# The expert weights of a second feed-forward block, laid out in DRAM as four pieces of a partition's row in place of one

## The chip, the core and the metric

One core of a Trainium2 chip runs the whole program in one launch. The metric is device time in microseconds (us). The core has five engines that run side by side and meet only at semaphores: TensorE (PE; its weight loads are PEld), VectorE (DVE), ScalarE (ACT), GpSimd (POOL) and SyncE (SP). DMAs are issued from a queue of SP (q1 in the profile), of ACT (q10) or of POOL (q0); all of them are carried out by the same 16 DMA engines. A DMA over 128 partitions gives each DMA engine 8 partitions.

## The reference

Two layers, each an attention block and a mixture of experts. Only the second mixture is touched. For 2048 rows `x` of 256 numbers it computes

```python
logits = silu(x @ rw1 + rb1) @ rw2 + rb2
k_logits, k_index = top_k(logits, 2)
k_prob = softmax(k_logits)
for e in range(8):
    we = sum(where(k_index == e, k_prob, 0))
    out += we[:, None] * (silu(x @ w1[e] + b1[e]) @ w2[e] + b2[e])
```

with `w1[e]` of 256 x 1024 and `w2[e]` of 1024 x 256, all in float32. "First layer weights" below are `w1` and `b1`.

## The kernel before

The second mixture is the last stage of the program. The router's table sorts the 4096 pairs of row and expert into 39 tiles (`NT1`) of up to 128 rows; a tile belongs to one expert. The first 8 tiles are those of the experts 0 to 7; which expert each of the other 31 belongs to is read from the table at run time.

For each tile:

- GpSimd gathers its 128 rows of 1 KB from DRAM by an indirect DMA (`fetch`, line 1354) into one of four buffers, four tiles ahead.
- SyncE loads the expert's first layer weights (`load_up`, line 1503) into one of two buffers `W1`: 128 partitions of 8224 bytes, 1028 KB. Of these 2056 floats a partition, 2048 are `w1` and 8 are `b1`. The load of tile i+2 goes into the buffer of tile i, so it waits until ScalarE has finished tile i (line 1498; the bias columns are read from the same buffer). From the ninth tile on SyncE then reads the expert's number into a register, which is the address of the load.
- TensorE transposes the gathered rows (line 333), multiplies by `w1` in two halves of 16 matmuls (`up`, line 457), and by `w2`, which lies in SBUF for all eight experts (`down_parts`, lines 483 to 486). The order on TensorE is fixed: up of half c, transposes of the next tile, down of half c-1.
- ScalarE applies silu with the bias (line 1213), VectorE splits the result into a high and a low part (lines 951, 953) and later adds the bias of the second layer and weighs the rows (lines 976 to 978).
- GpSimd adds the tile's 128 rows to the output in DRAM by an indirect accumulating DMA (`give`, line 1361). Two tiles can hold the same row, so each such scatter waits until the one before it has landed. GpSimd's order is: give of tile i, fetch of tile i+4.

In DRAM the weights of expert e are rows e*128 to e*128+127 of an array of 2056 columns, so a partition's 8224 bytes are one contiguous run, and SyncE's DMA copies rows to partitions.

The first mixture has the same structure with tiles of 2 MB and 1 MB of weights (`wide` is then `WS`), and gives rows out by a plain scatter into `yd`.

Of the kernel before, what the change touches and what calls it, by code (L numbers as in the profile page):

```python
# [15 lines left out]
P = 128  # L16
# [6 lines left out]
E = 8  # L23
# [53 lines left out]
def build(nc, cst, x, ctx_2048, plen, kmask, g_xattn, g_ffn, W_in, b_in, g_res, g_init, rw0, rb0, w01, w02,  # L77
          att_b, rw1, rb1, rw2, rb2, w11, w12, b12, out):
    es = ExitStack()
    with es:  # L80
# [11 lines left out]
        def placed(name, shape, at, dt=F32):  # L92
            return nc.alloc_sbuf_tensor_at(name, shape, dt, offset=arena + 4 * at)[:, :]

        def sem(name):
            return es.enter_context(nc.semaphore(name))
# [22 lines left out]
        W1 = [placed(f"W1{i}", [P, 2056], x_at + 2056 * i) for i in range(2)]  # L119
# [11 lines left out]
        def scratch(name, rows):  # L131
            return nc.dram_tensor(name, [rows, D], F32, kind="Internal").ap()


        dep_d, xn0, xn1, yd = (scratch(n, r) for n, r in (
            ("dep_d", NK * P), ("xn0", P + T), ("xn1", P + T), ("yd", P + T)))
# [3 lines left out]
        def sm(n):  # L140
            at[0] += n
            assert at[0] <= SMN, at[0]
            return SM[:, at[0] - n:at[0]]
# [11 lines left out]
        tile, lane, tabp, row = sm(2 * NC), sm(2 * NC), sm(40), sm(2 * NC)  # L155
# [16 lines left out]
        zero = Z1[:, 3584:3840]  # L172
# [15 lines left out]
        def w2_half(s, raw=False):  # L188
# [25 lines left out]

        d_plen, d_cst, d_ck, d_v, d_first, d_small = (sem(n) for n in ("d_plen", "d_cst", "d_ck", "d_v", "d_first", "d_small"))
        d_x = [sem(f"d_x{g}") for g in range(4)]
        d_zero = [sem("d_zero0"), sem("d_zero1")]
        d_dep = [sem(f"d_dep{i}") for i in range(2)]
        d_dg = [sem(f"d_dg{i}") for i in range(4)]
        d_xn = [[sem(f"d_xn{l}{i}") for i in range(4)] for l in range(2)]  # L220
        d_up = [[sem(f"d_up{l}{i}") for i in range(2)] for l in range(2)]
# [14 lines left out]
        v_xn, t_xn, a_xt, t_lg = sem("v_xn"), sem("t_xn"), sem("a_xt"), sem("t_lg")  # L236
        v_la, a_ex, v_oh, t_rank, v_slot, t_tab, v_tab, v_eid = (
            [sem(f"{n}{l}") for l in range(2)] for n in ("v_la", "a_ex", "v_oh", "t_rank", "v_slot", "t_tab", "v_tab", "v_eid"))
        v_flag, t_flag, v_mbh, v_ka, t_ka = (sem(n) for n in ("v_flag", "t_flag", "v_mbh", "v_ka", "t_ka"))

        t_tr, a_tr, t_up, t_down, v_y = (
            [sem(f"{n}{l}") for l in range(2)] for n in ("t_tr", "a_tr", "t_up", "t_down", "v_y"))
# [27 lines left out]
        def landed(i, slots):  # L270
            return 16 * (i // slots + 1)
# [51 lines left out]
        def _(e):  # L323
# [90 lines left out]
            def tables(l):  # L414
                nt, cc = (NT0, NT1)[l], NC * (1 + l)
                lanes, _, vals = slot_table(l)
                for q in range(cc):
                    if q % 8 == 0:
                        e.wait_ge(v_slot[l], q // 8 + 1)
                    t = e.matmul(PB[6][:, 0:3 * nt + 3], lanes[:, q, :], vals[:, q, :, :].rearrange("p s t -> p (s t)"),  # L420
                                 start=q == 0, stop=q == cc - 1)
                t.then_inc(t_tab[l], 1)
# [731 lines left out]
        def _(e):  # L1154
# [2 lines left out]
            e.wait_ge(v_pad, 2)  # L1157
            e.dma_start(CK[0:REM, 12, :], ctx_2048[12 * P:S2, 0:D]).then_inc(d_ck, 16)
            e.wait_ge(p_set, 1)
            for l, buf in ((0, xn0), (1, xn1)):  # L1160
                e.dma_start(buf[0:P, :], zero).then_inc(d_zero[l], 16)


            trash = [WS[0][:, 0:D], WS[0][:, D:2 * D]]
# [156 lines left out]
        def _(e):  # L1321
# [28 lines left out]
            def experts(l, nt, xn, into, **add):  # L1350
                def fetch(i):
                    if i >= 4:
                        e.wait_ge(t_tr[l], bank_of["xt", l, i - 4])
                    e.indirect_dma_start(FXL[i % 4], None, xn, bass.IndirectOffsetOnAxis(  # L1354
                        ap=tabi[:, i:i + 1].bitcast(U32), axis=0)).then_inc(d_xl[l][i % 4], 16)

                def give(i):
                    e.wait_ge(v_y[l], i + 1)
                    if i:
                        e.wait_ge(d_y[l][(i - 1) % 2], landed(i - 1, 2))  # L1360
                    e.indirect_dma_start(into, bass.IndirectOffsetOnAxis(ap=tabi[:, i:i + 1].bitcast(U32), axis=0),  # L1361
                                         FY[i % 2], None, **add).then_inc(d_y[l][i % 2], 16)

                e.wait_ge(v_tab[l], 1)
                for z in d_zero:
                    e.wait_ge(z, 16)
                for i in range(4):
                    e.wait_ge(d_xn[l][i], landed(NC - 1, 4))
                for i in range(4):
                    fetch(i)  # L1370
                if l == 1:
                    w2_low(14)
                    w2_low(15)
                for i in range(nt):
                    give(i)
                    if i + 4 < nt:
                        fetch(i + 4)

            def w2_low(s):
                e.wait_ge(a_wh[1], s + 1)  # L1380
                e.tensor_tensor(w2_half(s)[:, :, 1, :], w2_half(s, raw=True)[:, :, 1, :],
                                w2_half(s)[:, :, 0, :].bitcast(F32), ALU.subtract).then_inc(p_wl, 1)

            experts(0, NT0, xn0, yd)


# [66 lines left out]
            for s in range(14):  # L1453
                w2_low(s)
            e.wait_ge(d_res, 64)
            experts(1, NT1, xn1, out, compute_op=ALU.add)
            for i in range(2):
                e.wait_ge(d_y[1][i], landed(NT1 - 1 - (NT1 - 1 - i) % 2, 2))
# [3 lines left out]
        def _(e):  # L1462
# [23 lines left out]
            def experts(l, nt, w_up, w_down, free):  # L1486
                up_n = 4 * FF if l == 0 else 2 * FF + 8
                wide = WS if l == 0 else W1
                regs = {}

                def row(i, n):
                    return bass.ds(regs[i] * n, n) if i >= E else slice(i * n, i * n + n)

                def load_up(i):
                    if i >= 2:
                        e.wait_ge(t_up[l], (2 - l) * 2 * (i - 1))
                        if l == 1:
                            e.wait_ge(a_h, 4 * (i - 1))
                    if i >= E:
                        if i == E:  # L1500
                            e.wait_ge(v_eid[l], 1)
                        regs[i] = e.value_load(eidi[0:1, i:i + 1], min_val=0, max_val=E - 1)
                    e.dma_start(wide[i % 2][:, 0:up_n], w_up[row(i, P), :]).then_inc(d_up[l][i % 2], 16)

                def load_down(i):
                    if i >= 2:
                        e.wait_ge(v_wl, 2 * (i - 2) + 2)
                    e.dma_start(WS[i % 2][:, 4096:6144], w_down[row(i, P), :]).then_inc(d_down[i % 2], 16)

                def load_whole(k):  # L1510
                    x = W2_ORDER[k]
                    e.dma_start(W2G[E - 1 - x].rearrange("p (j s n) -> p j s n", j=8, s=2)[:, :, 1, :],
                                w_down[row(x, P), :].rearrange("p (j n) -> p j n", j=8)).then_inc(d_w2[k % 4], 16)

                if l == 1:
                    for k in range(4):
                        load_whole(k)
                    free()
                    load_up(0)
                    e.dma_start(B2, b12.partition_broadcast(P)).then_inc(d_bias, 16)  # L1520
                    e.wait_ge(t_hr, 32)
                    for i in range(4):
                        e.wait_ge(d_xn[1][i], landed(NC - 1, 4))
                    for k in range(4, E):
                        load_whole(k)
                    e.wait_ge(t_tab[1], 1)
                    for i in range(1, nt):
                        load_up(i)
                    return

                for i in range(2):
                    free(i)
                    load_up(i)
                    load_down(i)
                for c in range(1, 2 * nt + 1):
                    i = c // 2
                    if c % 2:
                        if i + 2 < nt:
                            load_up(i + 2)
                    elif i + 1 < nt:  # L1540
                        load_down(i + 1)
# [104 lines left out]
```

## Time and profile before

| | us |
|---|---|
| median of 3 runs | 1243.98 (1239.08 to 1245.86) |
| the profiled execution | 1242.3 |
| its span, first to last instruction | 1240.5 |

The profile is of one execution. "Busy" is the time in which an engine carries out instructions; "idle before" a group is the time in which its engine did nothing just before them, with what ended it. A DMA's "us to landing" runs from its issue to the semaphore update that tells of its last byte. In a window, the share of a DMA queue is the time that its packets took, over 16 engines; shares can exceed 100% by the packets that end after the window.

### The profile page before, as it was taken

How to read it: one execution, taken by the hardware profiler on the slowest of the kernel's cores; microseconds unless marked ns; L12 is line 12 of the kernel's file. 1: busy time of each engine (PE TensorE's matmuls, PEld its weight loads, DVE VectorE, ACT ScalarE, POOL GpSimd, SP SyncE). 2: the span in 40 equal slices, each digit the busy share in tenths (PEclk: the TensorE clock that was granted, in tenths of full speed). 3: DMA queues.
4: the chain of work that ended last, by engine and by line, in shares of the span. 5: the costliest groups of instructions: out<-in, count | busy, mean ns of one | idle time of the engine just before them, and what ended most of it. 6: DMA issues, size and time to landing. Idle time of an engine off the chain costs nothing.

```text
span 1240.5 us, 20677 instructions
## 1 busy us (share of the span) xinstructions
PE 1097.6 (88%) x7126; PEld 828.5 (67%) x7126; DVE 789.7 (64%) x1815; ACT 524.3 (42%) x1129; POOL 522.6 (42%) x515
## 2 busy tenths in 40 slices
PE   4865999999968799999999999999953999999995
PEld 3665999999955444545545454535732999999994
DVE  5765767666659886766758676753147555565553
ACT  4111434443311355556555565565450333333331
POOL 1241111111104375756667575674263343434332
PEclk9956999999986899999999999999975999999998
DMA  6254877788831000000000000004341566666662
GB/s 223 72 170 170 323 308 291 305 320 332 339 139 69 1 1 1 1 18 1 1 1 18 1 2 18 1 31 139 121 136 51 159 178 210 181 204 203 181 208 58
DMA packets 51219, 160.71 MB, mean 130 GB/s; under 512 B 7435, under 2 KB 36493, under 8 KB 40109
## 3 DMA queue, kind: packets, MB, share of 16 engines
q1 hardware_dynamic: 38590, 138.42, 30.8%
q0 software_dynamic: 10464, 18.36, 5.7%
q10 hardware_dynamic: 2062, 2.60, 0.6%
q8 instruction: 60, 0.98, 0.3%
q14 instruction: 43, 0.34, 0.1%
HBM read 142.97 MB, written 16.38 MB: 128 GB/s over the span
## 4 chain that ended last, share of the span: by engine, by line
PE 67%; DMA 10%; DVE 10%; issue 6%; ACT 3%; POOL 2%; SPq 1%; DVEq 0%; ACTq 0%; POOLq 0%
PE PQ L457 20%; DMA out<-Z,SI 8%; PE PB L603 7%; PE PQ L588 7%; PE PB L570 5%; DVE Z L1042 4%; PE PB L593 4%; PE PB L503 3%; PE PB L333 3%; PE PB L484 3%; PE PQ L570 2%; PE PB L502 2%; PE PB L483 1%; PE PQ L644 1%; PE PQ L646 1%
## 5 line engine op out<-in xcount | busy, mean ns | idle before, releaser
L1042 DVE TENSOR_REDUCE Z<-PB 128x1 f32<-128x402 f32 x319 | 171.9, 566 | 72.0 <-PE PB L570 70.7
L588 PE MATMUL PQ<-QS,KS 128*128 128x512 f32 x416 | 173.6, 433 | 3.4 <-ACT Z L1286 2.0
L457 PE MATMUL PQ<-Z,WS 128*128 128x128 f32 x1472 | 173.8, 277 | 0.5 <-ACT Z L1198 0.5
L457 PEld LDWEIGHTS PQ<-Z,WS 128*128 128x128 f32 x1472 | 172.3, 194 | 2.2 <-ACT Z L1198 0.9
L1213 ACT ACTIVATE Z<-PQ,W 128x128 f32<-128x128 f32 x312 | 89.0, 368 | 162.7 <-PE PQ L457 162.7
L457 PEld LDWEIGHTS PQ<-Z,W 128*128 128x128 f32 x1248 | 152.6, 193 | 6.9 <-issue 3.0
L457 PE MATMUL PQ<-Z,W 128*128 128x128 f32 x1248 | 153.9, 277 | 2.6 <-issue 2.2
L588 PEld LDWEIGHTS PQ<-QS,KS 128*128 128x128 f32 x416 | 77.2, 189 | 101.7 <-issue 66.2
L1286 ACT ACTIVATE Z<-PQ 128x512 f32<-128x512 f32 x208 | 109.8, 603 | 81.7 <-PE PQ L588 81.6
L1286 ACT ACTIVATE WS<-PQ 128x512 f32<-128x512 f32 x208 | 109.7, 604 | 81.5 <-PE PQ L588 81.4
L570 PE MATMUL PB<-KS,QS 128*128 128x402 f32 x319 | 119.6, 385 | 15.6 <-DVE Z L1042 6.6
L1042 DVE TENSOR_REDUCE Z<-PQ 128x1 f32<-128x402 f32 x193 | 106.7, 566 | 36.3 <-PE PQ L570 35.5
L1361 POOL DMA_INDIRECT out<-Z,SI x39 | 62.7, 1607 | 158.0 <-DMA out<-Z,SI 134.1
L1448 POOL TENSOR_TENSOR WS<-WS,Z 128x512 f32<-128x512 f32 x80 | 104.5, 1334 | 38.8 <-ACT Z L1286 38.8
L1361 POOL DMA_INDIRECT yd<-Z,SI x23 | 22.7, 987 | 205.3 <-DVE Z L973 205.3
L570 PEld LDWEIGHTS PB<-KS,QS 128*128 128x128 f32 x319 | 62.0, 195 | 41.4 <-DVE Z L1042 27.2
L1354 POOL DMA_INDIRECT Z<-xn,SI x62 | 61.2, 988 | 60.9 <-issue 36.6
L570 PE MATMUL PQ<-KS,QS 128*128 128x402 f32 x193 | 74.8, 405 | 6.6 <-DVE Z L1068 2.4
L1223 ACT ACTIVATE QS<-WS 128x1024 fp32r<-128x1024 f32 x46 | 48.6, 1057 | 72.9 <-PE PB L503 56.1
L951 DVE CAST HP<-Z 128x256 fp32r<-128x256 f32 x78 | 25.5, 327 | 79.8 <-ACT Z L1213 79.8
L503 PE MATMUL PB<-QS,AU 128*128 128x512 f32 x184 | 69.6, 406 | 0.0
L484 PE MATMUL PB<-W2F,HP 128*128 (+1 forms) x156 | 61.0, 413 | 0.0
(306 smaller groups left out, 2101.9 us busy)
## 6 DMA issues: line engine op xcount, KB each, us to landing
WS<-in_w SPq DMA_DIRECT2D x23, 2048.0 KB, 7.9
W<-in_w SPq DMA_DIRECT2D x39, 1028.0 KB, 5.2
WS<-in_w SPq DMA_DIRECT2D x23, 1024.0 KB, 7.3
W2G<-in_w SPq DMA_DIRECT2D x8, 1024.0 KB, 9.4
xn<-WS SPq DMA_DIRECT2D x32, 128.0 KB, 1.8
X<-in_x SPq DMA_DIRECT2D x4, 512.0 KB, 11.7
WS<-yd SPq DMA_DIRECT2D x4, 512.0 KB, 5.5
out<-X SPq DMA_DIRECT2D x4, 512.0 KB, 2.8
```

Source lines behind the costliest of these rows:

```text
L457: t = e.matmul(bank[:, j * P:j * P + P], w[:, k, o:o + P], FXT[i % 2][:, k * P:k * P + P], start=k == 0, stop=k == 1)
L484: t = e.matmul(PB[6 + i % 2], hh[:, j * P:j * P + P], both, start=first, stop=n == 1 and j == 3)
L503: t = e.matmul(PB[6 + i % 2], HA[:, j * P:j * P + P], W2P[n][:, j, :, :].rearrange("p s n -> p (s n)"), start=first, stop=last)
L570: e.matmul(PB[b][:, 0:PIECE], q[:, h, t4 * P:t4 * P + P], KS[:, 4 * hf + h, s * PIECE:(s + 1) * PIECE], start=True, stop=True).then_inc(t_ ...
L588: e.matmul(PB[g % 3], KS[:, 4 * (n % 2) + hh, kc * P:kc * P + P], QS[n % 2][:, hh, :], start=True, stop=True).then_inc(t_s, 1)
L603: e.matmul(PB[6][32 * hh:32 * hh + 32, :], V[:, kc, (4 * hf + hh) * 32:(4 * hf + hh) * 32 + 32], PT[(g + hh) % 16], start=kc == 0, stop=kc ...
L1042: e.tensor_reduce(MP[j % 2][:, i:i + 1], PB[bank_of["pc", r]][:, 0:PIECE], AX.X, ALU.max).then_inc(v_pc, 1)
L1213: t = e.activation(FS[c % 4][:, j * P:j * P + P], PB[c % 4][:, j * P:j * P + P], ACT.Silu, bias=W1[i % 2][:, o:o + 1])
L1286: e.activation(PT[g % 16], PB[g % 3], ACT.Exp).then_inc(a_p, 1)
L1354: e.indirect_dma_start(FXL[i % 4], None, xn, bass.IndirectOffsetOnAxis(ap=tabi[:, i:i + 1].bitcast(U32), axis=0)).then_inc(d_xl[l][i % 4], 16)
L1361: e.indirect_dma_start(into, bass.IndirectOffsetOnAxis(ap=tabi[:, i:i + 1].bitcast(U32), axis=0), FY[i % 2], None, **add).then_inc(d_y[l][ ...
L1448: e.tensor_tensor(acc, acc, PT[g % 16], ALU.add).then_inc(p_acc, 1)
```

## The change

The array of an expert is cut into four blocks of 514 columns, which lie one behind the other: 4 x 128 rows of 514 floats (2056 bytes). The host makes the array so. SyncE's DMA of a tile then takes 512 rows, and puts the four rows of a partition side by side in `W1`; the buffer holds the same bytes as before. The first mixture's loads are as they were. Besides, the two DMAs that clear the first rows of two scratch arrays share one semaphore (GpSimd waits for 32 once, in place of 16 twice), and two semaphores that nothing used are gone.

```diff
-        d_zero = [sem("d_zero0"), sem("d_zero1")]
+        d_zero = sem("d_zero")
...
-        v_flag, t_flag, v_mbh, v_ka, t_ka = (sem(n) for n in ("v_flag", "t_flag", "v_mbh", "v_ka", "t_ka"))
+        v_flag, t_flag, v_ka = (sem(n) for n in ("v_flag", "t_flag", "v_ka"))
...
-            for l, buf in ((0, xn0), (1, xn1)):
-                e.dma_start(buf[0:P, :], zero).then_inc(d_zero[l], 16)
+            for buf in (xn0, xn1):
+                e.dma_start(buf[0:P, :], zero).then_inc(d_zero, 16)
...
-                for z in d_zero:
-                    e.wait_ge(z, 16)
+                e.wait_ge(d_zero, 32)
...
-                    e.dma_start(wide[i % 2][:, 0:up_n], w_up[row(i, P), :]).then_inc(d_up[l][i % 2], 16)
+                    if l == 0:
+                        e.dma_start(wide[i % 2][:, 0:up_n], w_up[row(i, P), :]).then_inc(d_up[0][i % 2], 16)
+                    else:
+                        e.dma_start(W1[i % 2].rearrange("p (c n) -> p c n", c=4),
+                                    w_up[row(i, 4 * P), :].rearrange("(c p) n -> p c n", p=P)).then_inc(d_up[1][i % 2], 16)
...
         "w11": np.concatenate([blocks(L1_ffn_w1, 2), np.asarray(L1_ffn_b1).reshape(E, 8, P).transpose(0, 2, 1)
-                               .reshape(E * P, 8)], axis=1),
+                               .reshape(E * P, 8)], axis=1).reshape(E, P, 4, 514).transpose(0, 2, 1, 3).reshape(-1, 514),
```

## Rows read from the trace of the kernel before

**Rows 1.** Page: each engine's busy time, and the chain that ended last.

```profile
PE 1097.6 (88%) x7126; PEld 828.5 (67%) x7126; DVE 789.7 (64%) x1815; ACT 524.3 (42%) x1129; POOL 522.6 (42%) x515
PE 67%; DMA 10%; DVE 10%; issue 6%; ACT 3%; POOL 2%; SPq 1%; DVEq 0%; ACTq 0%; POOLq 0%
```

**Rows 2.** Windows of the second mixture: length, busy per engine, PEclk, DMA share, GB/s.

```profile
1062.00:1116.00 54.00, 53.51 (x406) 50.30 (x405) 32.09 (x90) 20.44 (x72) 21.05 (x16) 1.00 0.66 197
1116.00:1170.00 54.00, 53.43 (x401) 49.82 (x400) 31.94 (x88) 20.44 (x72) 20.76 (x16) 1.00 0.66 196
```

**Rows 3.** Waits of PE, 1007 to 1241: total us, times, longest.

```profile
PE PQ L457 <- issue: 2.2, 3, 1.1
PE PB L483 <- issue: 1.2, 4, 0.4
PE PB L483 <- DVE ZR L953: 0.3, 1, 0.3
```

**Rows 4.** Timeline of PE and SP: up's first matmuls of two tiles, and a load.

```profile
1061.77 1.50 PE L457 MATMUL PQ<-Z,W 128*128 128x128 f32 x12
1068.37 1.83 PE L457 MATMUL PQ<-Z,W 128*128 128x128 f32 x15
1062.53 0.34 SPq L1503 DMA_DIRECT2D W<-in_w  x1
```

**Rows 5.** The same, of the last tile.

```profile
1210.91 0.34 SPq L1503 DMA_DIRECT2D W<-in_w  x1
1217.44 0.79 PE L457 MATMUL PQ<-Z,W 128*128 128x128 f32 x5 [0.53 <-issue]
```

**Rows 6.** Line L1503, 1003 to 1241, and single loads: first, the slowest, last.

```profile
L1503 SPq DMA_DIRECT2D W<-in_w x31: 337/338/348, 1007.9 to 1210.9; - x31
DMA to landing us min/median/max: 4.9/5.2/7.1
...
DMA to landing us min/median/max: 5.6/5.6/5.6
...
DMA to landing us min/median/max: 7.1/7.1/7.1
...
DMA to landing us min/median/max: 6.4/6.4/6.4
```

**Rows 7.** DMA, 970 to 971: packets of one load alone.

```profile
DMA packets 48, 0.39 MB, mean 395 GB/s; under 512 B 0, under 2 KB 0, under 8 KB 0
q1 hardware_dynamic: 48, 0.39, 93.5%
```

**Rows 8.** DMA, 860 to 865: loads in pieces of 1 KB.

```profile
DMA packets 1759, 1.77 MB, mean 354 GB/s; under 512 B 32, under 2 KB 1759, under 8 KB 1759
q1 hardware_dynamic: 1759, 1.77, 109.6%
```

**Rows 9.** Line L1465: four loads of 512 pieces of 1 KB; durations of the issue, ns.

```profile
L1465 SPq DMA_DIRECT2D X<-in_x x4: 433/719/3142, 1.2 to 3.2; - x4
```

**Rows 10.** DMA, 967 to 1212: queues over 245 us.

```profile
q1 hardware_dynamic: 5191, 37.96, 46.7%
q0 software_dynamic: 6720, 9.18, 17.4%
```

**Rows 11.** DMA, 4.3 to 5.5 and 7 to 9: two queues with pieces of 1 KB.

```profile
q10 hardware_dynamic: 296, 0.31, 90.6%
q1 hardware_dynamic: 18, 0.00, 1.7%
...
q10 hardware_dynamic: 372, 0.38, 53.6%
q1 hardware_dynamic: 376, 0.37, 52.9%
```

**Rows 12.** Gathers (L1354): landing in 955 to 965; number and landing in 967 to 1212.

```profile
DMA to landing us min/median/max: 2.7/2.9/4.2
...
L1354 POOL DMA_INDIRECT Z<-xn,SI x35: 977/983/1227, 975.0 to 1206.4; - x35
...
DMA to landing us min/median/max: 2.9/4.3/6.6
```

**Rows 13.** Scatters (L1361): landing in 967 to 1212, in 1212 to 1241.

```profile
DMA to landing us min/median/max: 3.9/6.0/8.4
...
DMA to landing us min/median/max: 3.7/4.4/6.6
```

**Rows 14.** Timeline: transposes that came late for their gather; the last scatters.

```profile
1171.65 0.44 PE L333 MATMUL PB<-CT,Z 128*128 128x128 f32 x2
1172.51 0.38 PE L483 MATMUL PB<-W2F,ZR 128*128 x1 [0.42 <-issue]
...
1223.78 1.75 POOL L1361 DMA_INDIRECT out<-Z,SI  x1 [3.33 <-DVE Z L978]
1229.46 1.54 POOL L1361 DMA_INDIRECT out<-Z,SI  x1 [3.93 <-DMA out<-Z,SI]
```

## The prediction

> **What bounds the kernel now.** I read the page first: TensorE is busy for 88% of the span and carries 67% of the chain that ended last [rows 1]. The change touches only the last stage, 955 to 1240 us, so the rest of the argument is about that stage. Its windows come second: in 54 us TensorE is busy for 53.5, at the full clock of 2.4 GHz, and the DMA engines are busy for two thirds of the time [rows 2]. So there are almost no holes on TensorE to win. Third, TensorE's waits: from 1007 on they sum to 3.7 us (2.2 + 1.2 + 0.3) [rows 3]. That is all that any speed of DMAs can give back in the stage, apart from its end.
>
> Then the load itself. Two neighbouring tiles start their first matmul at 1061.77 and 1068.37, a period of 6.60 us; the load that the second of these needs is issued at 1062.53 [rows 4]. So a load has 1068.37 - 1062.53 = 5.84 us. The last tile shows what a late one does: issued at 1210.91, landed 6.4 us later, and TensorE goes on at 1217.44, about 0.1 us after the landing, having stood for 0.53 us [rows 5, 6]. A landing of up to 5.74 us is therefore free, and each tenth above is paid. The median landing is 5.2 us, with 4.9 and 7.1 as ends [rows 6]: the load is off the path by half a microsecond. Asked one by one (31 loads from the ninth tile on; the first, the slowest and the last stand in [rows 6]), 19 land within 5.2 us, nine take 5.3 to 5.6 us (5.4 in the mean), and three take 6.4, 6.4 and 7.1. These three are the three waits of 2.2 us in all at line 457 [rows 3]. The chain of waits names the scatters for 8% of the whole span, but TensorE worked on beside them; they cost it time only where the gather behind a scatter came too late, 0.42 us at 1172 [rows 14].
>
> **The change, part by part.** Bytes are the same; each of the 16 DMA engines gets 32 pieces of 2056 bytes in place of 8 of 8224.
>
> *The transfer.* In a microsecond with nothing but a load, 48 packets took 93.5% of 16 engines: 0.935 x 16 / 48 = 0.312 us a packet, 2.49 us for 8 [rows 7]. In pieces of 1 KB, 1727 packets (1759 less the 32 small ones of semaphores) took 1.096 x 5 x 16 = 87.7 us: 0.051 us each [rows 8]. On the line through these two, 2056 bytes cost 0.051 + 1032 x (0.312 - 0.051) / 7200 = 0.088 us, and 32 of them 2.82 us: +0.33 us a load. The ends are 0 (the bytes alone set the time) and, at the price of 1 KB pieces, 64.25 x 0.051 = 3.26, +0.77. I take +0.33, since both rows are of this very path, DRAM to SBUF from SP's queue.
>
> *The issue.* A load of 512 pieces held SP for 0.43 us where nothing was queued ahead, one of 128 pieces holds it for 0.34 [rows 6, 9]: +0.09 us. Ends: 0 and, by the median of the queued ones, +0.38. SP has nothing else to do in this stage, so only the load itself is later by it.
>
> *Who gets in between.* POOL's queue takes 17.4% of 245 us, in which 35 gathers lie: 0.174 x 245 / 35 = 1.22 us a tile on each DMA engine for a gather and a scatter [rows 10, 12]. Today a scatter lands in 6.0 us beside loads and 4.4 without, a gather in 4.3 against 2.9 [rows 12, 13], so they do wait for a load. With pieces four times smaller some of their packets can pass before the load's last one, and the load is later by what passes: between 0 and 1.22 us. The start of the program shows how two queues share: for 1.2 us after it had been served first, ACT's queue moved 296 pieces of 1 KB, about 18 on each DMA engine, while SP's moved 18 small ones in all; after that they alternate, 372 against 376 [rows 11]. If a served queue has some 18 pieces under way, only the last 14 of a load's 32 are open to others, and only where a scatter was ready in the load's first half. I take +0.1 us.
>
> Sum for a load: 0.33 + 0.09 + 0.1 = +0.5 us. The 19 loads up to 5.2 end at 5.7 at most, still free. The nine go from 5.4 to 5.9 in the mean, 0.2 past the free 5.74: 1.8 us. The three late ones lose 0.5 more each: 1.5 us. Together 3.3 us. The first eight tiles have more room (no register is read before the load) and pay nothing; the very first load is issued long before the stage.
>
> *What comes back.* Scatters and gathers that pass part of a load land earlier. That is worth the wait behind a late gather, 0.42 us and the slower restart, at most 0.9 and I take 0.5 [rows 14]. The end gains nothing: no load is under way there, the last scatter but one is released by VectorE at 1223.78, and the last waits for it [rows 14].
>
> *The semaphores.* The merged pair guards scratch rows cleared at the start of the program, and GpSimd waits for it long after; one wait instruction less per mixture. Nothing, with both ends below 0.1 us; its cover is the wait for the router's table that stands ahead of it.
>
> Net 3.3 - 0.5 = +2.8 us. On the profiled execution's own 1242.3 us that is 1245.1. The median of the runs stands 1.7 above that execution, so the forecast on its scale is **1246.8 us**.
>
> Ends: with no price anywhere and every wait of TensorE gone, 1244.0 - 3.7 = 1240.3. With all upper ends, 0.77 + 0.38 + 1.22 = 2.4 us more a load; then each tile waits, and as a load is issued two tiles ahead of its use, half of the excess is paid per tile: mean landing 5.3 + 2.4 = 7.7, (7.7 - 5.74) / 2 x 31 = 30 us, 1274.
>
> **The rivals.**
>
> *Slower: the load loses the DMA engines to scatters and gathers.* If the queues alternate piece by piece as soon as both are ready (372 against 376 [rows 11]), a load with a scatter and a gather beside it takes on a good part of their 1.22 us. With +0.6 in place of +0.1 the rise is 1.0 us: mean landing 6.3, (6.3 - 5.74) / 2 x 31 = 8.7 us, and the loads above the mean add some 2: about 10.5 with the 0.5 taken back, 1254.5 us. It decides from a rise of about 0.7 us on, where the 19 quick loads lose their cover too. For it: the even shares [rows 11]. Against it: the 18 pieces that one queue had ahead, more than half a load.
>
> The Trainium skill, "DMA: Bandwidth & Descriptors", section "Queues, rings and completion order", says that a DMA engine drains a whole packet, typically 9 to 17 descriptors, from one ring before it turns to the next. A load of 8 pieces would then be one turn, and one of 32 two to four turns with the scatter in between; that is this rival's mechanism, and would give its time. The profile's rows agree with turns of that order at most in the 18 pieces at the start.
>
> *Faster: scatters and gathers pass and the load has room for them.* Landing stays within 5.74 us for nearly all loads; the late gather and the waits for HP and ZR halves behind it go. At most -3.7, and 1241.5 as its likeliest. For it: landings of scatters beside loads are 1.6 us longer than alone [rows 13]. Against it: TensorE waits hardly at all for gathers, and the price of more packets has to be nothing.
>
> *Nothing: the pieces are joined again*, since their places in SBUF are side by side, and packets of 8224 bytes remain: 1244.0.
>
> **How the numbers follow.** The forecast has 0.58, the slower rival 0.22, the faster 0.14, nothing 0.06. A change of 0.5%, 6.2 us, is about what a measurement of this kernel can tell from none: below 1237.8 is faster, above 1250.2 slower. TensorE's waits do not reach 6.2 us, so faster has only what measurement scatter gives, 0.06. Slower is the slower rival and the upper tail of the forecast, whose own range is 1243 to 1251: 0.27. The rest is no change, 0.67. The range that holds 8 in 10 is 1240 to 1256.
>
> **What would show it.** Right: about 512 larger packets a load in the stage (some 16,000 more in all), a median landing of line 1503's successor near 5.7 us, PE's waits at line 457 near 5 us in place of 2.2, scatters' median landing under 6.0, period still 6.60 us where nothing waits. Wrong in the transfer: a load alone that lands later than 5.3. Wrong in the sharing: median landing beyond 6.0 and waits at every tile. Wrong altogether: a packet count as before, or a different length of the stages before 955 us.

## The result, and the profile after

The changed kernel takes 1254.4 us (median of 5 runs, 1250.5 to 1255.2), the kernel before 1243.5 (5 runs, 1239.1 to 1245.9). The ratio is 1.0096, 95% interval 1.0071 to 1.0122: 11 us slower. The profiled execution is one of 1254.43 us with a span of 1252.6.

The page first. TensorE's busy time has grown by 5 us; its share of the chain went from 67% to 76%, DMA's from 10% to 2% [rows 1]. So the end is now set by TensorE together with its own waits, and no longer by scatters.

```profile
PE 1102.5 (88%) x7126; PEld 827.7 (66%) x7126; DVE 788.6 (63%) x1815; ACT 524.9 (42%) x1129; POOL 522.9 (42%) x515
PE 76%; DVE 10%; issue 6%; ACT 3%; POOL 2%; DMA 2%; SPq 1%; ACTq 0%; DVEq 0%; POOLq 0%
q1 hardware_dynamic: 53566, 138.42, 31.2%
```

Where the 12.1 us of span lie: line 457's matmuls in the stage begin at 962.7 and end at 1235.8, against 960.5 to 1222.4 before. 2.2 us are older than the stage (see `sem_only`), 11.2 are inside it, and the end after the last matmul is 1.3 us shorter, since the last scatter no longer waits for the one before it but for VectorE.

```profile
L457 PE MATMUL PQ<-Z,W x1248: 270/275/581, 962.7 to 1235.8; 128*128 128x128 f32 x179
```

And GpSimd's last two scatters, from the timeline, the answer to [rows 14]:

```profile
1237.15 1.54 POOL L1361 DMA_INDIRECT out<-Z,SI  x1 [3.86 <-DVE Z L978]
1241.64 1.54 POOL L1361 DMA_INDIRECT out<-Z,SI  x1 [2.95 <-DVE Z L978]
```

TensorE's waits from 1010 us on in the changed kernel, beside [rows 3] of the kernel before:

```profile
PE PQ L457 <- issue: 9.2, 7, 1.9
PE PB L483 <- issue: 1.6, 4, 0.5
PE PB L483 <- DVE ZR L953: 0.3, 1, 0.3
```

The waits for a load went from 2.2 us in three to 9.2 us in seven. The counterpart of [rows 6] tells why: line 1505, loads from 1003 us on, then single loads (the ninth tile's, the slowest, the last).

```profile
L1505 SPq DMA_DIRECT2D W<-in_w x32: 368/378/393, 1003.2 to 1224.8; - x32
DMA to landing us min/median/max: 5.1/5.6/7.8
...
DMA to landing us min/median/max: 6.2/6.2/6.2
...
DMA to landing us min/median/max: 7.8/7.8/7.8
...
DMA to landing us min/median/max: 5.4/5.4/5.4
```

Asked one by one, 20 of the 31 loads land within 5.9 us, five take 6.2 to 6.4, and six take 7.4 to 7.8. Before, three of 31 passed 6 us. The median moved by 0.4 us, the tail by much more.

The slowest load shows one way in which a load becomes late. It is issued at 1143.73, 1.15 us after a scatter. TensorE goes on at 1151.62 after 1.90 us of waiting, and its 16 matmuls then take 3.65 us in place of 1.95: in the stretch from 1151.6 on the granted clock is 0.57 of full speed, so for most of it the lower of the two levels, 1.2 GHz, after TensorE had done nothing for 1.9 us.

```profile
1142.58 1.59 POOL L1361 DMA_INDIRECT out<-Z,SI  x1 [2.53 <-DVE Z L978]
...
1143.73 0.38 SPq L1505 DMA_DIRECT2D W<-in_w  x1
...
1151.62 3.65 PE L457 MATMUL PQ<-Z,W 128*128 128x128 f32 x16 [1.90 <-issue]
```

The window behind it (length, PE busy, PEclk, DMA share, GB/s):

```profile
1151.60:1155.60 4.00, 3.98 (x20) 0.57 0.90 270
```

While it is on its way the DMA queues share as follows, in three windows of the changed kernel's profile: 1144.7 to 1146.4, 1146.4 to 1147.8, 1148.7 to 1150.

```profile
q1 hardware_dynamic: 115, 0.24, 66.1%
...
q1 hardware_dynamic: 133, 0.27, 57.8%
q0 software_dynamic: 123, 0.13, 55.5%
...
q1 hardware_dynamic: 101, 0.18, 35.8%
q0 software_dynamic: 46, 0.13, 25.7%
q8 instruction: 1, 0.02, 4.7%
```

115 pieces, 7.2 on each DMA engine, go before POOL's first packet. From then on the two queues take turns, 133 packets against 123. At the end an instruction fetch of 16 KB sits on one DMA engine (4.7% of 16 x 1.3 us, 0.98 us) among the load's last pieces.

That is not how most loads of the changed kernel fare. Here is one of 5.5 us, issued only 0.50 us after its scatter, with the queues in 1061.5 to 1064.9 and in 1064.9 to 1066.5:

```profile
1060.02 1.62 POOL L1361 DMA_INDIRECT out<-Z,SI  x1 [2.50 <-DMA out<-Z,SI]
...
1060.52 0.38 SPq L1505 DMA_DIRECT2D W<-in_w  x1
...
q1 hardware_dynamic: 449, 0.92, 91.0%
...
q0 software_dynamic: 189, 0.26, 73.6%
q1 hardware_dynamic: 79, 0.13, 21.9%
```

More than 440 of its 512 pieces pass with nothing of POOL's queue between them. So it was in 22 of the 31 loads: by the order of the packets in the trace, 28 to 31 of the 32 pieces on a DMA engine began before POOL's first one. The slowest load of the kernel before, issued 0.08 us after its scatter, is of this kind too (1042.3 to 1045.4, 1045.4 to 1046.4):

```profile
q1 hardware_dynamic: 114, 0.94, 91.9%
...
q0 software_dynamic: 116, 0.13, 74.0%
q1 hardware_dynamic: 29, 0.12, 28.0%
```

114 of its 128 pieces pass first. Its last piece began 4.8 us after the issue; it landed at 7.1, and the last of its 16 semaphore writes began just as an instruction fetch of 0.96 us ended (1047.4).

What sets the loads apart is how long before them the scatter was issued. In eight of the 31 this was 1.04 to 1.36 us. There POOL's first packet came after 0 to 13 of the load's pieces on a DMA engine, and the eight landed in 6.8 us in the mean, the other 23 in 5.8. Five of the six loads past 7 us had a fetch of 16 KB while they were under way; three of the six are of the eight, one (issued at 1128.81) is late by its semaphore writes as the one of before, and why the last two, issued at 1031.54 and 1038.18, were late is not worked out. Of the 9.2 us of waits, 5.8 come behind four of the eight. In the kernel before only one of the 31 loads had its scatter so far ahead (1.1 us); it landed in 5.5. What moves the scatter ahead of the load was not looked into.

The scatters and gathers gained nothing by the change: scatters land in 4.0/5.9/8.7 us (least, median, most) and gathers in 2.9/4.4/6.9, against 3.9/6.0/8.4 and 2.9/4.3/6.6 [rows 12, 13].

### The profile page after: what moved, and what is told of

Read it like the earlier page. It is cut to its first block, busy times and chain, and to the rows that moved or that the text cites. A ratio compares the mean times of both kernels' runs of the same rounds, so it can differ in the third digit from the quotient of the medians.

```text
span 1252.6 us, 20676 instructions
## 1 busy us (share of the span) xinstructions
PE 1102.5 (88%) x7126; PEld 827.7 (66%) x7126; DVE 788.6 (63%) x1815; ACT 524.9 (42%) x1129; POOL 522.9 (42%) x515
## 3 DMA queue, kind: packets, MB, share of 16 engines
q1 hardware_dynamic: 53566, 138.42, 31.2%
## 4 chain that ended last, share of the span: by engine, by line
PE 76%; DVE 10%; issue 6%; ACT 3%; POOL 2%; DMA 2%; SPq 1%; ACTq 0%; DVEq 0%; POOLq 0%
PE PQ L457 25%; PE PB L603 7%; PE PQ L588 7%; PE PB L484 6%; PE PB L570 5%; DVE Z L1042 4%; PE PB L593 4%; PE PB L333 4%; PE PB L503 3%; PE PB L483 3%; PE PQ L570 2%; PE PB L502 2%; PE PQ L644 1%; PE PQ L646 1%; PE PQ L645 1%
## 5 line engine op out<-in xcount | busy, mean ns | idle before, releaser
L457 PE MATMUL PQ<-Z,W 128*128 128x128 f32 x1248 | 156.5, 280 | 9.8 <-issue 9.2
L1361 POOL DMA_INDIRECT out<-Z,SI x39 | 62.3, 1599 | 168.1 <-DMA out<-Z,SI 108.7
L1361 POOL DMA_INDIRECT yd<-Z,SI x23 | 22.7, 987 | 205.4 <-DVE Z L973 205.4
L1354 POOL DMA_INDIRECT Z<-xn,SI x62 | 61.9, 998 | 60.9 <-issue 35.9
L1447 POOL TENSOR_TENSOR WS<-WS 128x512 f32<-128x512 f32 x40 | 51.0, 1304 | 24.3 <-ACT WS L1286 24.3
```

The lines of the kernel that those rows point to most:

```text
L457: t = e.matmul(bank[:, j * P:j * P + P], w[:, k, o:o + P], FXT[i % 2][:, k * P:k * P + P], start=k == 0, stop=k == 1)
L1447: e.tensor_tensor(acc, acc, PT[g % 16], ALU.add).then_inc(p_acc, 1)
```

## The experiments

Twelve kernels ran, four to a chip, each beside the kernel before. Ratios are to the kernel before on the same chip (its medians there were 1240.0, 1240.7 and 1242.7 us); "waits" are those of TensorE for a load in the profiled execution, "landing" is the median of all loads of the stage (`noscat_four`'s trace lacks some of the records that it needs). The kernels with `noscat` in their name leave out the scatters of the middle tiles, those with `nopool` the gathers besides.

The expectations speak of three theories. A: traffic of POOL's queue gets in between a load's pieces. B: the pieces cost more by themselves, by their number or by their places in DRAM. C: instruction fetches of 16 KB make the late loads.

| kernel | median us | ratio (95%) | waits us (times) | landing |
|---|---|---|---|---|
| before | 1243.5 | | 2.2 (3) | 5.2 |
| changed | 1254.4 | 1.0096 (1.0071 to 1.0122) | 9.2 (7) | 5.6 |
| layout_only | 1257.1 | 1.0152 (1.0115 to 1.0188) | 8.4 (10) | 5.7 |
| near4 | 1258.2 | 1.0154 (1.0134 to 1.0175) | 12.6 (15) | 6.4 |
| pieces2 | 1245.7 | 1.0039 (1.0015 to 1.0064) | 8.0 (9) | 5.2 |
| pieces8 | 1263.8 | 1.0200 (1.0178 to 1.0221) | 19.1 (17) | 7.2 |
| noscat_whole | 1242.7 | 1.0021 (1.0004 to 1.0037) | 1.6 (3) | 5.3 |
| noscat_four | 1244.7 | 1.0037 (1.0012 to 1.0062) | 3.6 (5) | - |
| ring3_whole | 1241.6 | 1.0005 (0.9992 to 1.0017) | none | 5.2 |
| ring3_four | 1244.6 | 1.0030 (1.0007 to 1.0053) | none | 5.5 |
| nopool_whole | 1237.3 | 0.9970 (0.9951 to 0.9989) | 1.4 (3) | 4.9 |
| nopool_four | 1240.0 | 0.9981 (0.9963 to 0.9999) | 2.9 (4) | 5.2 |
| delay_whole | 1250.7 | 1.0106 (1.0057 to 1.0154) | 4.4 (5) | 5.1 |
| sem_only | 1240.5 | 1.0002 (0.9985 to 1.0018) | none | 5.1 |

**The parts alone.** `sem_only` is the changed kernel with the load and the layout of before:

```diff
-                        e.dma_start(W1[i % 2].rearrange("p (c n) -> p c n", c=4),
-                                    w_up[row(i, 4 * P), :].rearrange("(c p) n -> p c n", p=P)).then_inc(d_up[1][i % 2], 16)
+                        e.dma_start(wide[i % 2][:, 0:up_n], w_up[row(i, P), :]).then_inc(d_up[1][i % 2], 16)
```

> The kernel before with the merged semaphore of the cleared rows alone. All theories: no difference, 1238 to 1245 us, with the whole loss in the layout.

1.0002: no difference. `layout_only` is its mirror, the kernel before with the new layout and load.

> The kernel before with the four-piece layout and load alone; the two semaphores of the cleared rows stay apart. Both theories of the loads (A: scatters, gathers and instruction fetches get in between the pieces; B: the pieces cost more by themselves, by their number or their places in DRAM) expect the whole loss: 1253 to 1255 us, as the changed kernel (1254.4). Only if the merged semaphore had a part in it would this stay near 1244 to 1249.

1.0152, 1257.1 us against 1240.0: the whole loss and, on this chip, some more. The layout alone makes the kernel slower. The 2.2 us by which the stage began later in the profile are most likely a difference between executions: `sem_only` has the changed kernel's code up to the stage, and there line 457's matmuls begin at 958.3, against 962.7 in the changed kernel and 960.5 in the kernel before.

**Places in DRAM or pieces.** `near4` keeps a partition's row together and pads each piece by 8 bytes, so that four pieces stay.

```diff
-                                    w_up[row(i, 4 * P), :].rearrange("(c p) n -> p c n", p=P)).then_inc(d_up[1][i % 2], 16)
+                                    w_up[row(i, P), :].rearrange("p (c n) -> p c n", c=4)[:, :, 0:514]).then_inc(d_up[1][i % 2], 16)
```

> Four pieces of 2056 bytes a partition as in the changed kernel, but a partition's pieces lie in one row of DRAM as before, 8 bytes apart (so that they are not joined). Theory A: the same number of pieces, so the same time, 1252 to 1256 us, and 512 larger packets a load. Theory B by the places in DRAM: 1243 to 1247 us.

1.0154, with 20064 packets in its queue in the stage. Putting the pieces side by side again wins nothing back, so their distance in DRAM is not the harm. It is not quite a clean comparison: issuing such a load takes SyncE 0.54 us in place of 0.38. In this profile the sharing is at its plainest: every one of the 31 loads from the ninth tile on was issued 1.0 us or more after its scatter, POOL's packets were being moved when the load's began, scatters land in 4.0 us in the median and loads in 6.4.

**More and fewer pieces.** `c=2` (2 x 4112 bytes) and `c=8` (8 x 1028 bytes) in place of `c=4`, with the array to match.

> The changed kernel with two pieces of 4112 bytes a partition (16 a DMA engine). Theory A: a queue that is being served has about 8 pieces under way when another comes in, so half of the load is open to others: 1246 to 1251 us, with single loads beyond 7 us but fewer of them. Theory B by number of pieces: 8 x 0.014 = 0.1 us more a load, 1244 to 1245, and no load that lands beyond those of before.

> The changed kernel with eight pieces of 1028 bytes a partition (64 a DMA engine). Theory A: nearly the whole load is open to others and each load takes on up to 1.2 us of scatter and gather beside 0.8 us more of its own: 1262 to 1275 us. Theory B: 0.8 us more of its own alone, landings near 6.0 with little spread, 1250 to 1256 us.

Ratios 1.0039, 1.0096 to 1.0152, 1.0200 for two, four, eight pieces: the loss grows with their number. `pieces8` lies in the range of theory A. `pieces2`, at 1245.7 us, lies just below A's 1246 to 1251 and just above B's 1244 to 1245, so its time does not decide; its loads do. Its median landing is that of before, 5.2 us, and the loss is in single loads (9 of 31 past 6 us, up to 7.7), as A has it and a price per piece (0.1 us) does not. Eight of its loads came 1.0 us or more after their scatter; they landed in 6.6 us in the mean, the others in 5.2. In `pieces8` 30 of 31 loads came so late after their scatter, and the typical load itself lands at 7.2 us.

The same split in the other profiles, means of the loads from the ninth tile on:

| | scatter 1.0 us or more ahead | other loads |
|---|---|---|
| whole rows (before, sem_only, ring3_whole, delay_whole) | 5.55 us (9 loads) | 5.22 us (114) |
| four pieces (changed, layout_only, ring3_four) | 6.73 us (16) | 5.75 us (71) |

So behind an earlier scatter a load in four pieces a partition lands about 1 us later than the others, a load of whole rows 0.3 us later; nine loads are few, though. Loads also came into that position more often: one of 31 with whole rows, eight with two and with four pieces, 30 with eight. Why is not shown.

TensorE's waits from 1005 us on, of `pieces2` and of `pieces8`, and the landing of `pieces8`'s loads in 965 to 1225:

```profile
PE PQ L457 <- issue: 8.0, 9, 1.8
```

```profile
PE PQ L457 <- issue: 19.1, 17, 1.9
```

```profile
W<-in_w SPq DMA_DIRECT2D x35, 1028.0 KB, 7.2
```

**Who gets in between.** Without the scatters of the middle tiles:

```diff
+                    if not given(l, i):
+                        return
...
+        def given(l, i):
+            kept = [j for j in range(i % 2, i + 1, 2) if l == 0 or j < 4 or j > 34]
+            return len(kept) if kept[-1] == i else 0
```

> The kernel before, with whole rows of 8224 bytes, without the scatters of tiles 4 to 34 (their rows do not reach the output; the first four and the last four remain, gathers are as they were). Both theories: loads land in about 5.1 us, the waits of TensorE at line 457 fall from 2.2 to under 1.5 us; 1238 to 1243 us.

> The changed kernel, with four pieces, without the scatters of tiles 4 to 34 (their rows do not reach the output). Theory A (others get in between the pieces): with the scatters gone, most of the loss goes: landings near 5.4 us, the gather alone adds to a load, 0 to 4 us slower than noscat_whole. Theory B (the pieces cost more by themselves): the loss of 11 us over noscat_whole stays. If what gets in is mainly the instruction fetches of 16 KB, single landings above 7 us stay as well.

TensorE's waits in `noscat_whole` are 1.6 us, a little above the 1.5 expected.

And without the gathers too (`if i + 4 < nt and l == 0: fetch(i + 4)`, with TensorE's wait for them gone from the fifth tile on):

> The kernel before, whole rows, without the scatters of tiles 4 to 34 and without the gathers from the fifth tile on (those tiles compute on old rows; only loads and instruction fetches use the DMA engines in the middle of the stage). Theory A: landings 4.9 to 5.0 us for all loads that no instruction fetch meets, 1239 to 1243 us, as noscat_whole or a little faster.

> The changed kernel, four pieces, without the scatters of tiles 4 to 34 and the gathers from the fifth tile on (those tiles compute on old rows). Theory A (what POOL's queue puts in between): landings 5.3 to 5.4 us, no difference to nopool_whole beyond 1 us. Theory C (instruction fetches of 16 KB make the late loads): single landings above 6.5 us stay and cost 2 us or more over nopool_whole. Theory B (the pieces by themselves): +11 us over nopool_whole.

`nopool_whole`, at 1237.3 us, is faster than the 1239 to 1243 expected.

With all traffic four pieces cost 11 us in one comparison and 17 in the other; without the scatters 2.0 us (1244.7 - 1242.7), without POOL's queue 2.6 (1240.0 - 1237.3), and in both of these pairs the two intervals overlap. Most of the loss needs the scatters, as theory A has it. Theory A had allowed at most 1 us for the last pair, and theory C is not refuted for these 2 us: single loads of up to 6.8 us stay, against 6.4 in `nopool_whole`, and the typical load lands 0.3 us later. The two shares were not told apart. The loads past 7 us are gone in `nopool_four`, and in the changed kernel most of them had a fetch besides. TensorE's waits of `nopool_four`:

```profile
PE PQ L462 <- issue: 2.9, 4, 0.9
```

**Room for the load.** A third buffer of 8224 bytes a partition lies in columns that nothing uses any more in the stage; a load then has one tile, 6.6 us, more.

```diff
+        W1.append(placed("W12", [P, 2056], z_at + 4088))
+        RING = (2, 3)
...
-                            e.wait_ge(a_h, 4 * (i - 1))
+                            e.wait_ge(a_h, 4 * (i + 1 - RING[l]))
```

> The kernel before (whole rows, semaphore merged) with three buffers for the first layer weights, so that a load has 6.6 us more. Both theories: no wait of TensorE for a load is left (2.2 us before): 1 to 4 us faster than before, unless scatters and gathers, now free of the load's phase, become late.

> The changed kernel with three buffers, four pieces. If the loss is only that loads land later than their 5.8 us, it goes altogether: same as ring3_whole within 2 us, although landings stay at 5.6 us and more. If four pieces cost something else too (slower matmuls, later gathers), a part of the 11 us stays.

TensorE's waits from 1005 us on, of `ring3_four` (its line 485 is line 483 of before, its 335 line 333):

```profile
PE PB L485 <- issue: 2.6, 6, 0.5
PE PB L335 <- DMA Z<-xn,SI: 0.5, 2, 0.2
PE PB L485 <- DVE ZR L955: 0.3, 1, 0.3
```

No wait for a load is left, the pieces are as they were, and the loss falls from 11 us or more to 3 (1244.6 against 1241.6). So about three quarters of it or more came through TensorE waiting for loads. What the last 3 us are is not settled; the two intervals overlap (up to 1.0017, from 1.0007). In the profiles, line 485 and the gathers make TensorE wait 3.4 us in `ring3_four` and 1.9 in `ring3_whole`. `ring3_whole` was expected 1 to 4 us faster than the kernel before and is not: the 2.2 us of waits that it takes away are within what can be measured. No kernel of this study beats the kernel before clearly and computes all of the output.

**An even delay.** To weigh the prediction's arithmetic, whole rows and an extra register read on SyncE ahead of each load.

> The kernel before, whole rows, with the expert's number read twice before each load from the ninth tile on: every such load is issued some 0.75 us later and shares the DMA engines as before. It tests the price of an even delay: a load has then 5.1 us in place of 5.84, its median landing is 5.2. The working of the prediction (half of what is over, per tile, and the late ones beside) gives 6 to 8 us more than before, with short waits at most of the 31 tiles. If an even delay costs nearly nothing, the loss of the changed kernel has another source than the landing of its loads.

The delay is less than expected. The loads are issued 7.92 us after the first matmul of the tile two before, in the median, against 7.35, so 0.57 us later. The median of the runs is 8 us above before, and the ratio says 13 (7 to 19). The profiled execution, a quick one with a span of 1247.7, has five waits for loads:

```profile
PE PQ L457 <- issue: 4.4, 5, 1.2
PE PB L483 <- issue: 1.0, 3, 0.4
PE PB L483 <- DVE ZR L953: 0.3, 1, 0.3
```

By the working of the prediction a delay of 0.57 us costs 9 x 0.23 for the nine loads at 5.4 and 3 x 0.57 for the late ones, 3.8 us. The runs say at least 7. So that sum is too low even for an even delay. The trace shows where a part went: seven of the 31 loads were now issued 1.27 us or more after a scatter, against one before. They landed in 5.7 us in the mean, two of them at 6.4 and 6.6; the others in 5.2. A delay so moves loads into the position in which scatters go first.

## Why the prediction came out as it did

The time of 1254.4 us lies in the range of 1240 to 1256, near its upper end, but not because the working was right. The forecast itself was 1246.8 and "no change", with 0.67 for it; by the prediction's own border, 1250.2 us, the kernel is slower, for which it gave 0.27. The time is that of the slower rival (1254.5 us, chance 0.22), and so is the mechanism where it bites. But that rival had nearly every load 1 us later, and what happened is a few loads much later.

- *The view of what bounds the stage* held: TensorE at 6.60 us a tile, a load with 5.84 us, free up to 5.74, each load past that paid. `ring3_four` confirms it.
- *The transfer* held. In 973 to 974, a load alone, 194 packets took 105.4% of a microsecond on 16 engines, 0.087 us each, against 0.088 worked out. The loads of the second and third tile, which POOL's queue hardly touches, land in 5.4 and 5.2 us, 0.4 later than before (4.9 and 4.8), as 0.33 + 0.09 had it.

```profile
DMA packets 194, 0.40 MB, mean 399 GB/s; under 512 B 0, under 2 KB 0, under 8 KB 194
q1 hardware_dynamic: 194, 0.40, 105.4%
```

- *The issue* was less than forecast: 0.38 us in place of 0.43.
- *Who gets in between* is the step that failed. It took +0.1 us for every load, on the reading that a served queue has some 18 pieces ahead [rows 11]. No such single number holds in this stage. In 22 of 31 loads 28 or more of the 32 pieces went first, fewer were open than forecast; in the eight loads with a scatter 1.04 us or more ahead it was 0 to 13, and those landed 1 us later than the rest. The working asked what is ready in the load's first half, and not what was issued before the load.
- *One rise for all loads* was the second half of the error. The median rose by 0.4 us, close to the 0.5 of the forecast. The mean of the 31 rose by 0.7, from 5.3 to 6.0, because six loads landed at 7.4 to 7.8. The sum dealt with the three late loads of before as if they stayed three. For the same reason the prediction's sign of wrong sharing, a median beyond 6.0 and waits at every tile, did not show.
- *What comes back*: nothing was seen. The late gather at 1172 went, but the waits at line 483 are 1.6 us, against 1.2 before.
- *The semaphores*: nothing, as said.
- *The count of pieces*: 53566 packets in SyncE's queue against 38590, so 14976 more, which is 39 loads x 384; the prediction's 16,000 was a slip.
- *Not in the working at all*: after the longest wait TensorE ran at half its clock for one group of matmuls, 1.7 us.

The Trainium skill's rule of turns ("DMA: Bandwidth & Descriptors", "Queues, rings and completion order": 9 to 17 descriptors from one ring before the next) gave the right sign. This case's traces do not bear its numbers out: where the queues shared, they did so about one for one (133 against 123 packets in 1.4 us), and where they did not, 28 pieces and more of one load went first.

## What to carry to other kernels

A load in many short pieces is more exposed to another queue's traffic that was issued before it. Here a load of four pieces a partition lost about 1 us to a scatter issued 1 us or more ahead, a load of whole rows 0.3 us, and neither let much in when the scatter was issued later than that. Where a load's landing is what TensorE waits for and scatters have time, long rows are right; whether short pieces help where the gather or scatter is the late one was not tried. Judge such a change by the slowest landings against the time that a load has, not by the median, and look at what else was issued in the microsecond before each load. A buffer more makes the question small.

## What the runs showed of the hardware that was not expected

- Pieces of 2056 bytes moved as fast as those of 8224 (399 against 395 GB/s in a microsecond of a load alone).
- Which queue goes first hung on a few tenths of a microsecond. With the scatter issued 0.9 us or less ahead of a load of 32 pieces on each DMA engine, 28 or more of them went before POOL's first packet; with 1.04 to 1.36 us, 0 to 13 did (changed kernel).
- A load can be late although its data are not: the one issued at 1041.38 in the kernel before began its last piece 4.8 us after the issue and landed at 7.1, its last semaphore write beginning as a fetch of 16 KB ended.
- A wait of 1.90 us on TensorE was followed by half the clock for one group of 16 matmuls (3.65 us in place of 1.95); the six others of 0.3 to 1.85 us in the same stage were not. The length of the wait does not decide it alone: in `near4` a wait of 2.04 us was followed by the full clock, and in `pieces8` one of 1.92 by half the clock for a part of the group (2.54 us) and two of 1.90 and 1.91 by the full one.
